# An encoder phase's borders put in another order on three engines, in a whole-model fp32 kernel

## What is computed

```python
for l in range(LAYERS):            # 6
    keys = concatenate([past, x], axis=1)            # one zero row in front
    q = x @ Wq.T + bq; k = keys @ Wk.T + bk; v = keys @ Wv.T + bv
    scores = einsum('bqhd,bkhd->bhqk', q, k) / sqrt(HEAD_DIM)
    attn = softmax(where(valid, scores, neg), axis=-1)
    o = einsum('bhqk,bkhd->bqhd', attn, v) @ Wo[l].T + bo[l]
    x = _ln(x + o, ln1_g[l], ln1_b[l])
    ff = gelu(x @ W1[l].T + b1[l]) @ W2[l].T + b2[l]
    x = _ln(x + ff, ln2_g[l], ln2_b[l])
```

## Time and profile before

| what | us |
|---|---|
| median of 3 runs | 865.48 (864.29 to 866.86) |
| the profiled execution, time | 864.54 |
| its span | 862.7 |
| PE busy, share of the span | 798.5 (93%) |
| DVE busy | 642.3 (74%) |
| ACT busy | 462.2 (54%) |
| POOL busy | 256.9 (30%) |

### The profile page before, as it was taken

One profiled execution on the slowest core, in us unless ns is written; L12 is line 12 of the kernel. 1 busy time (PEld: TensorE's weight loads), 2 busy tenths in 40 slices (PEclk: granted clock), 3 DMA queues, 4 the chain that ended last, 5 costly groups with the idle time before them and its releaser, 6 DMA issues.

```text
span 862.7 us, 15969 instructions
## 1 busy us (share of the span) xinstructions
PE 798.5 (93%) x5736; PEld 731.1 (85%) x5736; DVE 642.3 (74%) x1285; ACT 462.2 (54%) x820; POOL 256.9 (30%) x297
## 2 busy tenths in 40 slices
PE   5889899999999997999999999989999998979698
PEld 4788769999999987898898979879897997969466
DVE  5696593877788768778778787877878787765686
ACT  3385314433333345776775777677567667725421
POOL 0002100411111101641654364164436516422232
PEclk9899799999999998899999999999999999988889
DMA  5000936988888702000210210021021002200000
GB/s 180 1 1 4 401 95 233 336 318 319 315 318 319 285 1 101 26 13 13 99 36 12 67 67 1 12 97 36 12 79 55 0 12 97 101 1 1 0 1 29
DMA packets 18289, 88.33 MB, mean 102 GB/s; under 512 B 3121, under 2 KB 7473, under 8 KB 12241
## 3 DMA queue, kind: packets, MB, share of 16 engines
q1 hardware_dynamic: 18256, 87.90, 28.8%
HBM read 85.05 MB, written 2.84 MB: 102 GB/s over the span
## 4 chain that ended last, share of the span: by engine, by line
PE 42%; issue 27%; POOL 18%; DVE 9%; ACT 3%; DMA 1%; POOLq 0%; SPq 0%; DVEq 0%; ACTq 0%
PE bank L1084 13%; POOL W_L L1903 6%; PE bank L1121 5%; POOL arena L1888 4%; POOL HF_L L1947 4%; PE bank L1226 3%; POOL WQKV_L L1903 2%; PE bank L770 2%; PE bank L724 2%; PE bank L1130 2%; POOL SQ L1917 2%; PE bank L1402 2%; PE bank L1067 1%; PE bank L872 1%; DVE CN L1991 1%
## 5 line engine op out<-in xcount | busy, mean ns | idle before, releaser
L1084 PE MATMUL bank<-arena 128*128 (+1 forms) x1024 | 117.9, 274 | 0.5 <-ACT arena L1646 0.5
L1084 PEld LDWEIGHTS bank<-arena 128*128 128x128 f32 x1024 | 117.4, 192 | 0.7 <-ACT arena L1646 0.7
L1888 POOL TENSOR_TENSOR arena<-arena,srec 111x456 f32<-111x456 f32 x56 | 52.4, 963 | 129.4 <-DVE srec L2047 129.4
L770 PE MATMUL bank<-XHL,W_H 128*128 128x296 f32 x384 | 90.2, 314 | 0.0
L770 PE MATMUL bank<-XHL,WQKV_H 128*128 128x296 f32 x288 | 73.1, 327 | 6.3 <-DVE XHL L2488 4.9
L1947 POOL TENSOR_TENSOR HF_L<-arena,HF_H 128x296 fp32r<-128x296 f32 x48 | 43.8, 935 | 111.5 <-ACT HF_H L1803 111.5
L1903 POOL TENSOR_TENSOR W_L<-LW,W_H 128x256 fp32r<-128x256 f32 x96 | 70.1, 772 | 18.9 <-ACT W_H L1689 18.9
L770 PEld LDWEIGHTS bank<-XHL,W_H 128*128 128x128 f32 x384 | 66.0, 194 | 1.2 <-DVE XHL L2488 1.2
L1803 ACT ACTIVATE arena<-bank,vec 128x296 f32<-128x296 f32 x96 | 48.8, 509 | 23.0 <-PE bank L770 22.4
L2059 DVE TENSOR_SCALAR OB<-bank,lvec 96x148 f32<-96x148 f32 x144 | 51.2, 368 | 12.8 <-PE bank L840 10.4
L770 PEld LDWEIGHTS bank<-XHL,WQKV_H 128*128 128x128 f32 x288 | 49.3, 192 | 13.2 <-DVE XHL L2488 8.0
(11 more groups left out here) (260 smaller groups left out, 2080.9 us busy)
## 6 DMA issues: line engine op xcount, KB each, us to landing
arena<-ew_in SPq DMA_DIRECT2D x16, 2048.0 KB, 9.3
arena<-ew_in SPq DMA_DIRECT2D x16, 1024.0 KB, 6.7
LW<-lw_in SPq DMA_DIRECT2D x12, 1024.0 KB, 4.9
arena<-route SPq DMA_DIRECT2D x32, 185.0 KB, 3.4
LW<-lw_in SPq DMA_DIRECT2D x6, 768.0 KB, 4.4
fp_weights<-arena SPq DMA_DIRECT2D x1, 2048.0 KB, 6.4
arena<-fp_weights SPq DMA_DIRECT2D x1, 2048.0 KB, 7.1
arena<-patches_in SPq DMA_DIRECT2D x2, 864.0 KB, 8.3
```

What stands on the lines that cost most here:

```text
L770: last = mm(o, w, x, start=(i == 0), stop=(i == len(pairs) - 1))
L1084: last = mm(o[:, m * CAP:(m + 1) * CAP], w[:, kc, mi * P:(mi + 1) * P], xg(kc, e), start=(kc == 0), stop=(kc == C - 1))
L1888: nc.gpsimd.tensor_tensor(v, v, srec[0:QROWS, s:s + 2, :].unsqueeze(3).to_broadcast([QROWS, 2, C * JH, KEYS]), ALU.mult).then_inc(p_ready, 1)
```

## The change

It has four parts, all in the encoder's phases.

- **Products in pairs.** `two_products` takes the first two output banks of a stream together: the four XH matmuls of both, then the two XL matmuls of both. It is used for the two value products and for the first two hidden products.
- **Order on PE at the front.** Queries 0 now stand ahead of the first mean, with a wait for the residual of chunk 0 (it uses that bank); keys 1 now stand ahead of the mean square. In `down` the last three hidden blocks are done for output chunk 0, then for chunk 1.
- **Order at the end of a phase that has x and y.** On PE the first chunk of the second group's values stands ahead of the mean square. On DVE the gather of that chunk stands ahead of the reciprocal, and the other chunk's behind it.
- **Split of w1 on POOL.** It was the last work of a B phase, in one piece. Now it is in the A phase: four pieces ahead of `add_squares`, started only once x_ready shows that the low parts of the attention's stream are done, and four behind it, followed by w2's eight as before.

```diff
--- before.py
+++ after.py
@@ -760,23 +760,32 @@
...
-            def products(o, pairs, high_count=None, low_count=None):
+            def products(o, pairs):
                 for i, (w, x) in enumerate(pairs):
-                    if high_count is not None and i < 2 * C and i % 2 == 0:
-                        pe.wait_ge(xh_ready, chunk_count(high_count, i // 2))
-                    if low_count is not None and i == 2 * C:
-                        pe.wait_ge(x_ready, low_count)
                     last = mm(o, w, x, start=(i == 0), stop=(i == len(pairs) - 1))
...
-            def project_v(r, plan, h, pairs, high_count=None, low_count=None):
-                for c in range(C):
-                    key = ("w", 2 * h + c)
-                    free_bank(r, plan, key)
-                    products(bank_of(plan, key)[:, 0:NHALF], pairs(c), high_count if c == 0 else None,
-                             low_count if c == 0 else None).then_inc(filled["w"], 1)
+            def two_products(r, plan, keys, pairs, high_count, low_count):
+                for part in range(2):
+                    for key, all_pairs in zip(keys, pairs):
+                        o = bank_of(plan, key)[:, 0:NHALF]
+                        if part == 0:
+                            free_bank(r, plan, key)
+                        for i in (range(2 * C) if part == 0 else range(2 * C, 3 * C)):
+                            if key is keys[0] and part == 0 and i % 2 == 0:
+                                pe.wait_ge(xh_ready, chunk_count(high_count, i // 2))
+                            if key is keys[0] and i == 2 * C:
+                                pe.wait_ge(x_ready, low_count)
+                            last = mm(o, *all_pairs[i], start=(i == 0), stop=(i == 3 * C - 1))
+                        if part == 1:
+                            last.then_inc(filled[key[0]], 1)
+            def project_v(r, plan, h, pairs, high_count, low_count):
+                two_products(r, plan, [("w", 2 * h + c) for c in range(C)], [pairs(c) for c in range(C)],
+                             high_count, low_count)
@@ -1236,15 +1245,20 @@
...
+                    def up_pairs(m):
+                        return stream_pairs("w1", slice(m * P, (m + 1) * P), hy)
                     def up(*ms):
...
                             free_bank(ry, plan, key)
-                            cols = slice(m * P, (m + 1) * P)
-                            products(bank_of(plan, key)[:, 0:NHALF], stream_pairs("w1", cols, hy),
-                                     xa_count(ly, hy, 0) - skipped(ly, hy, 0) if m == 0 else None,
-                                     x_count(ly, hy, 0) - skipped(ly, hy, 0) if m == 0 else None
-                                     ).then_inc(filled["f1"], 1)
+                            products(bank_of(plan, key)[:, 0:NHALF], up_pairs(m)).then_inc(filled["f1"], 1)
+                    def up_first():
+                        two_products(ry, plan, [("f1", FM * hy + m) for m in range(2)], [up_pairs(m) for m in range(2)],
+                                     xa_count(ly, hy, 0) - skipped(ly, hy, 0),
+                                     x_count(ly, hy, 0) - skipped(ly, hy, 0))
@@ -1252,18 +1266,20 @@
...
                             free_bank(ry, plan, key)
-                        for m in range(FM):
-                            if m < FM // 2:
+                        tail = FM - 3
+                        order = [(m, c) for m in range(tail) for c in range(C)]
+                        order += [(m, c) for c in range(C) for m in range(tail, FM)]
+                        for m, c in order:
+                            if c == 0 and m < FM // 2:
                                 pe.wait_ge(hl_ready, low_count_of(ly, hy, m))
-                            else:
+                            elif c == 0:
                                 pe.wait_ge(hl_ready_pool, low_count_of(ly, hy, m - FM // 2))
-                            for c in range(C):
-                                parts = three("w2", m, slice(c * P, (c + 1) * P), HF_H[:, m, :], HF_L[:, m, :])
-                                for i, (w, moving) in enumerate(parts):
-                                    last = mm(bank_of(plan, keys[c])[:, 0:NHALF], w, moving,
-                                              start=(m == 0 and i == 0), stop=(m == FM - 1 and i == 2))
-                                if m == FM - 1:
-                                    last.then_inc(filled["f2"], 1)
+                            parts = three("w2", m, slice(c * P, (c + 1) * P), HF_H[:, m, :], HF_L[:, m, :])
+                            for i, (w, moving) in enumerate(parts):
+                                last = mm(bank_of(plan, keys[c])[:, 0:NHALF], w, moving,
+                                          start=(m == 0 and i == 0), stop=(m == FM - 1 and i == 2))
+                            if m == FM - 1:
+                                last.then_inc(filled["f2"], 1)
@@ -1289,6 +1305,10 @@
...
+                if x:
+                    if y:
+                        pe.wait_ge(proj_added, nth("p", 2 * hy, ry))
+                    queries_or_keys(0, "q")
                 if y:
@@ -1297,12 +1317,11 @@
...
                 if x:
-                    queries_or_keys(0, "q", "k")
-                    queries_or_keys(1, "q")
+                    queries_or_keys(0, "k")
+                    queries_or_keys(1, "q", "k")
                 if y:
...
                 if x:
-                    queries_or_keys(1, "k")
                     if entry:
@@ -1316,7 +1335,9 @@
...
                 for i in range(4):
-                    if y:
+                    if y and i == 0:
+                        up_first()
+                    elif y:
                         up(2 * i, 2 * i + 1)
@@ -1339,10 +1360,12 @@
...
                     gate_up(0, 0)
+                if x and y:
+                    values(rx, plan, 2 * hx + 1, (0,))
                 if y:
...
                 if x:
-                    values(rx, plan, 2 * hx + 1)
+                    values(rx, plan, 2 * hx + 1, (1,) if y else range(C))
                 else:
@@ -1894,14 +1917,18 @@
...
+            def split_part(name, lo, hi):
+                value, high, low = (t.rearrange("p c n -> p (c n)") for t in SPLIT[name][:3])
+                for at in range(lo, hi, LOW_COLS):
+                    cols = slice(at, at + LOW_COLS)
+                    last = nc.gpsimd.tensor_tensor(low[:, cols], value[:, cols], high[:, cols], ALU.subtract)
+                return last
             def split_weights(name, l):
-                value, high, low = (t.rearrange("p c n -> p (c n)") for t in SPLIT[name][:3])
                 pool.wait_ge(wh_ready[name], l + 1)
-                for lo in range(0, value.shape[1], LOW_COLS):
-                    cols = slice(lo, lo + LOW_COLS)
-                    last = nc.gpsimd.tensor_tensor(low[:, cols], value[:, cols], high[:, cols], ALU.subtract)
-                last.then_inc(wl_ready[name], 1)
+                split_part(name, 0, C * 3 * D if name == "qkv" else 2 * FM * P).then_inc(wl_ready[name], 1)
@@ -1936,9 +1963,14 @@
...
+                if y and y[0] == 0:
+                    pool.wait_ge(wh_ready["w1"], y[1] + 1)
+                    pool.wait_ge(x_ready, y[1] * 4 + 4)
+                    split_part("w1", 0, FM * P)
                 if y:
...
                     if y[0] == 0:
+                        split_part("w1", FM * P, 2 * FM * P).then_inc(wl_ready["w1"], 1)
                         split_weights("w2", y[1])
@@ -1952,7 +1984,7 @@
...
                     add_squares(y[1], 1, y[0])
-                if late_split(x):
+                if late_split(x) and late_split(x)[0] == "qkv":
                     split_weights(*late_split(x))
@@ -2046,9 +2078,9 @@
...
-            def gather_values(r, plan, g4, bias):
+            def gather_values(r, plan, g4, bias, chunks=range(C)):
                 h = g4 // 2
-                for c in range(C):
+                for c in chunks:
                     n = nth("o", 2 * g4 + c, r)
@@ -2644,10 +2676,13 @@
...
                     gather_values(rx, plan, 2 * hx, lambda c: lv(lx, "bqkv", 2 * C + c))
+                if x and y:
+                    gather_values(rx, plan, 2 * hx + 1, lambda c: lv(lx, "bqkv", 2 * C + c), (0,))
                 if y:
...
                 if x:
-                    gather_values(rx, plan, 2 * hx + 1, lambda c: lv(lx, "bqkv", 2 * C + c))
+                    gather_values(rx, plan, 2 * hx + 1, lambda c: lv(lx, "bqkv", 2 * C + c),
+                                  (1,) if y else range(C))
                 if y:
```

## The result

The changed kernel took 842.10 us (median of 4 runs, 840.31 to 847.08), the kernel before, run beside it, 864.88 (4 runs, 864.22 to 866.86). The ratio is 0.9737 with a 95% interval of 0.9714 to 0.9761: 22.8 us faster. The forecast was 850.0, with a range down to 844.5.

What follows compares the result with a forecast made beforehand. PE was taken to set the time, with 21 us of 416 idle in the encoder. Gains of 8.8 + 2.85 + 3.8 = 15.4 us took the median from 865.48 to 850.0 us; range 844.5 to 859.5.

Steps and rivals of the forecast that it cites:

- End of a phase: Eleven phase ends: third values chunk and its gather go earlier, removing DVE's idle times; 0.8 us each, 8.8 us.
- The rival in which the broadcast is late and gives everything back: At phase ends, root, gather and broadcast run 0.5 later, broadcast sets XD, gain is lost: 858.8 us; chance 0.20.
- Front of a B phase: Start of five B phases: earlier XL matmuls and keys 1 bring hidden products forward; 0.57 us each, 2.85 us.
- my upper bound: Front of a B phase: gain of at most 0.82 us, a whole product.
- Front of an A phase: Start of five A phases: XL takes 0.96 instead of 1.91, partly given back later; 0.76 us each, 3.8 us.
- the 2.47 less 0.8 of the sum: A phase: hidden products start 2.47 us earlier, of which 0.8 belongs to the end of the phase before.
- The first A phase, which I gave 0 at its front: Front of the first A phase: no XL stall there (5 stalls in 6 phases), so gain 0.
- A turn of the loop: Sign that the forecast is right: a turn takes about 72.2 us instead of 75.2.
- `down`: New order of the last three hidden blocks: 0, between 0.05 us gain and 0.8 us loss a phase.
- The start phase and the last one get 0: Start and last phases, each with one side only: slack on all engines, so gain 0.

## Why the prediction was right in direction and too high in time

**End of a phase: right in mechanism, a little small.** Forecast 0.8, measured 1.0: from the fourth score group to the next phase it is 20.30 us in an A phase and 20.23 in a B phase after, and 21.26 and 21.25 before, and undoing it costs 1.02 to 1.10. The idle times went whole. The term was mis-sized because I laid rows end to end: a triple of gathers "takes" 1.16, but the next instruction starts 1.08 behind its start (422.98 to 424.06), and behind the reciprocal of 0.16 the gather starts after 0.09. The rival in which the broadcast is late and gives everything back is out: the broadcast waits 0.17 us and is still ahead of XD.

**Front of a B phase: mis-sized.** Forecast 0.57, measured 0.82 (first product to hidden products 11.29, then 10.47), my upper bound. The relay from mean to mean square took 3.15 (2.65 to 5.80) where I had carried over 3.27 from an A phase.

**Front of an A phase: right, and slightly small.** XL takes 0.96 at the start, the pieces 0.73 to 0.77, and the hidden products come 1.64 us earlier relative to the first product, as the 2.47 less 0.8 of the sum had it (1.67). Of this 0.65 is given back, where I had 0.91: the XL there took 1.66 and not 1.91. Net 0.99 against 0.76. The kernel in which w2's pieces wait shows this cause by itself: 0.7 us come back. The first A phase, which I gave 0 at its front, lost 0.6 there: it never had the stall at the start, but it got the collision (5.31 us from hidden products to fourth score group, 4.66 before). With the end's 0.96 that makes the 0.36 of the table. A turn of the loop took 71.4 us, where I had forecast 72.2.

**`down`: right.** Forecast 0, measured 0.

**"The start phase and the last one get 0": this step failed.** The last phase gave 3.2 us, the rest 0.8 and the time up to the first A phase 0.9. The argument was that these have slack on all engines. It left out that the granted clock in the earlier trace rows is 1.00 only as far as 767 us. Behind that stood 0.70 and 0.56 in the kernel before, in a stretch where PE is the busy engine, so low clock there costs time. After the change the clock was 0.50 only from about 6 to 9 us behind the last phase's mean, instead of from about 0.5 to 14: the four matmuls of line 711 took 1.16 us, where they had taken 2.18. That the 3.2 us are the clock and not the new order follows from two relatives of the kernel after, the one with products one after the other and the one with the old split. They keep nearly all of the change, and their last phases take 26.31 and 26.28 us at a clock of 0.74, as in the kernel before. The rest's 0.8 goes with its clock too (0.94 and 0.92). The 0.9 ahead of the encoder is within what the traces scatter there, 354.05 to 360.28 us.

What brings the low clock earlier or later stays open. The filled gap speaks for PE's idleness ahead of the mean as one cause of the early fall. It doesn't explain why the kernel after, with nearly the same gap (2.01 and 2.09), keeps the clock for 6 us behind the mean, when the two relatives with a gap of 2.02 lose it within 1 us. Nor is it shown how much of it belongs to the change and how much to the single execution. The runs of the kernel after had a mean clock of 0.977 three times and 0.969 once (847.08 us), those of the kernel before mostly 0.966 to 0.974. But the kernel with w2's wait alone ran from 0.965 (844.17 us) to 0.975 (836.87).

How the 22.8 us of the medians divide: 19.3 are the phases, shown part by part. Single runs of both kernels at like mean clock differ by about that: some 865 and 847.1 us at 0.970 and 0.969, 860.46 and 840.3 to 843.5 at 0.976 and 0.977. The remaining 3.5 are the clock at the end of the program and scatter ahead of the encoder, which I can't part further. In the profiled executions the forecast was 849.1 and the time 840.31: of these 8.8 us, 3.9 are small terms in the phases, all but one of the same sign, and 4.9 the last phase, the rest and the start. In medians it took both to come out below 844.5 us: 864.88 less the phases' 19.3 is 845.6, and less the forecast's 15.4 and the 3.5 it is 846.0.

The parts undone one at a time add up to 1.02 + 0.69 + 0.07 + 0.43 = 2.2 in an A phase and 1.10 + 0.70 + 0.37 = 2.2 in a B phase, against 1.94 and 1.83 together: they overlap by about 0.3.

## What to carry to other kernels

At a phase border, give PE something that is ready ahead of each wait, and give the engine that feeds the next phase its next piece ahead of the one that waits for a relay: two idle times of half a microsecond, eleven times, were the largest part here. Where an engine's long stretch of small pieces slows another's short instruction, hold the pieces with a wait for that instruction. What it gives depends on what PE has to do meanwhile: the wait ahead of w1's pieces, where PE had other matmuls, gave 0.20 us an A phase, and the one ahead of w2's, which the change left out, 0.7. And when a sum is made over phases, read the granted clock of the stretches outside them as well, above all where the busy engine has just stood idle. In the traces here these stretches alone moved by about 4 us (88.99 to 93.11 us for the last phase and the rest) between kernels that do the same work in them.

## What I had not expected of the hardware

- The same gap of 2.0 to 2.1 us in PE's work is followed by nearly 14 us at 1.2 GHz in some kernels and by about 3 us, begun 6 us behind the mean, in others; between them the last phase differs by 3.2 us (26.27 and 23.09).
- Filling the gap in the kernel before with 20 small matmuls moved the fall to 4 us behind the mean and shortened it to 7 us, but didn't remove it.
- DVE instructions in a row start closer together than their own rows are long: the three gathers are 1.16 us long and 1.08 from the next one's start, the reciprocal 0.16 and 0.09.
- An XL that meets POOL's pieces isn't slowed by a fixed factor: 1.91, 1.66, 1.62, 1.51 (the hidden products' XL with the old front order) or 1.02 us, against 0.96 alone. The 1.02 was in the first A phase of the kernel before, at 365.24 with the pieces ending at 365.50.
